# Routing that scatters whole rows with their expert numbers, weights and targets, so that an expert reads its slots in one plain transfer

## What is computed

```python
x = x + jnp.tanh(g_xattn[0]) * _L0_xattn_ref(_layernorm(x, axis=-1), ctx_512, ...)
...
logits = x @ gate_w.T
topv, topi = jax.lax.top_k(logits, TOP_K)
rw = jax.nn.softmax(topv.astype(jnp.float32), axis=-1).astype(x.dtype)
W = jnp.zeros((N, E), x.dtype).at[jnp.arange(N)[:, None], topi].set(rw)
gu = jnp.einsum('nh,eih->nei', x, gu_w)
gate, up = (gu[..., :I], gu[..., I:])
inter = jax.nn.silu(gate) * up
inter_w = inter * W[:, :, None]
out = jnp.einsum('nei,ehi->nh', inter_w, dp_w)
```

## Time and profile before

| | us |
|---|---|
| median of 3 runs | 1684.83 |
| lowest, highest | 1680.01, 1685.89 |
| span of the profiled execution, first to last instruction | 1675.0 |
| between that span and the median of the runs | 9.8 |
| PE busy in the span | 1460.0 |
| DVE busy | 1118.3 |
| POOL busy | 967.6 |
| ACT busy | 677.6 |

### The profile page before, as it was taken

The page is one execution under the profiler, slowest core; times in us unless marked ns, Lnnn a source line. Parts: engine busy times, 40 slices in busy tenths (PEclk is TensorE's granted clock), DMA queues, the critical chain, the costliest instruction groups (busy, mean ns, idle before and its releaser), DMA issues.

```text
span 1675.0 us, 24705 instructions
## 1 busy us (share of the span) xinstructions
PE 1460.0 (87%) x7674; PEld 1183.0 (71%) x7674; DVE 1118.3 (67%) x2420; ACT 677.6 (40%) x1558; POOL 967.6 (58%) x997
## 2 busy tenths in 40 slices
PE   7998899999999999899999899745887888889884
PEld 5766787776787777687777687634777777778742
DVE  5777780588784388796189784543665676767386
ACT  3333670111772011484011372302665666666420
POOL 4654670277773266674267773365877776777321
PEclk9999999999999999999999999866998998999998
DMA  7898204555103665201655504335788999899596
GB/s 249 298 315 280 81 6 135 189 175 170 42 6 97 181 186 176 61 16 51 186 182 170 176 7 129 107 90 166 216 260 271 321 318 297 295 306 282 173 424 291
DMA packets 155974, 308.99 MB, mean 184 GB/s; under 512 B 37626, under 2 KB 73044, under 8 KB 154004
## 3 DMA queue, kind: packets, MB, share of 16 engines
q1 hardware_dynamic: 124100, 245.42, 45.0%
q0 software_dynamic: 31744, 61.99, 12.2%
HBM read 239.01 MB, written 70.43 MB: 185 GB/s over the span
## 4 chain that ended last, share of the span: by engine, by line
PE 53%; DVE 14%; issue 10%; POOL 7%; DMA 7%; ACT 4%; another core or an unknown queue 4%; SPq 1%; POOLq 0%; DVEq 0%; ACTq 0%
PE bank L722 14%; PE bank L724 13%; PE bank L723 13%; PE bank L820 6%; PE bank L846 3%; DMA p_in<-parts 3%; DVE q_sin L1135 2%; POOL parts L1825 2%; DVE q_rope L1131 2%; POOL x_g L1818 1%; DMA x_g<-xn_dram,t_rows 1%; POOL q_rope L1743 1%; PE bank L985 1%; ACT prob L1515 1%
## 5 line engine op out<-in xcount | busy, mean ns | idle before, releaser
L1743 POOL TENSOR_TENSOR q_rope<-q_rope,q_sin 128x448 f32<-128x448 f32 x192 | 218.0, 1164 | 149.4 <-DVE q_sin L1135 148.3
L1749 POOL TENSOR_TENSOR prob<-prob,row_inv 128x375 f32<-128x375 f32 x219 | 176.9, 814 | 105.1 <-DVE row_inv L1157 102.7
L1825 POOL DMA_INDIRECT parts<-y_sb,t_rows x140 | 161.0, 1150 | 84.1 <-ACT y_sb L1651 47.7
L1818 POOL DMA_INDIRECT x_g<-xn_dram,t_rows x140 | 158.0, 1129 | 50.7 <-issue 41.4
L1764 POOL DMA_INDIRECT table<-entry,pos_i x128 | 127.2, 993 | 97.0 <-DVE count L1245 66.3
L820 PE MATMUL bank<-q_rope,m_w 128*128 128x448 f32 x384 | 159.5, 552 | 13.9 <-DVE q_tl L1141 9.1
L1135 DVE TENSOR_TENSOR q_sin<-bank,sin_q 128x448 f32<-128x448 f32 (+1 forms) x256 | 158.1, 618 | 4.0
L1149 DVE TENSOR_REDUCE row_max<-bank 128x1 f32<-128x375 f32 x224 | 119.5, 535 | 41.2 <-PE bank L724 40.6
L846 PE MATMUL bank<-ident,prob 128*125 128x128 f32 x672 | 115.8, 283 | 21.2 <-POOL prob L1749 9.7
L1651 ACT ACTIVATE y_sb<-bank,t_rows 112x512 f32<-112x512 f32 (+5 forms) x140 | 91.4, 687 | 106.0 <-PE bank L724 49.2
L1515 ACT ACTIVATE prob<-bank,row_max 128x375 f32<-128x375 f32 x224 | 128.4, 574 | 9.9 <-DVE row_max L1149 9.4
(11 more groups left out here) (345 smaller groups left out, 4452.2 us busy)
## 6 DMA issues: line engine op xcount, KB each, us to landing
w_ex<-in_w_ex SPq DMA_DIRECT2D x64, 768.0 KB
p_in<-parts SPq DMA_DIRECT2D x14, 2048.0 KB, 16.8
m_w<-m_dram SPq DMA_DIRECT2D x48, 192.0 KB, 2.5
wq_s0h<-wq_dram SPq DMA_DIRECT2D x24, 256.0 KB
wq_s0l<-wq_dram SPq DMA_DIRECT2D x24, 256.0 KB
wq_s1h<-wq_dram SPq DMA_DIRECT2D x24, 256.0 KB
wq_s1l<-wq_dram SPq DMA_DIRECT2D x24, 256.0 KB
wcq_s0h<-wcq_dram SPq DMA_DIRECT2D x24, 192.0 KB
```

Of the source, the lines that this page charges most:

```text
L1743: pool.tensor_tensor(o[:, c, :], o[:, c, :], q_sin[:, c, :], ALU.add).then_inc(s_radd, 1)
L1749: pool.tensor_tensor(prob[i][:], prob[i][:], row_inv[:, i:i + 1].to_broadcast([P, L]), ALU.mult)\
L1818: pool.indirect_dma_start(x_g[x % NXE][0:size, t, :], None, xn2_dram, bass.IndirectOffsetOnAxis(ap=t_rows[x % NROW][0:size, t, 0:1].bitcas ...
L1825: pool.indirect_dma_start(parts, bass.IndirectOffsetOnAxis(ap=t_rows[x % NROW][0:size, t, 1:2].bitcast(I32), axis=0), y_sb[x % NY][t][0:si ...
```

## The change

`table`, the gathers and the table reads go. `slot_rows` in DRAM has 1792 slots for each expert, each a row of 544 words: the 512 channels, the token's eight expert numbers twice, its eight weights, and its eight rows in `parts` (counted from 1280). The routing writes these words into the row buffer (`rows`, three buffers and two `early_rows`) beside the normalised channels, and each of the 8 indirect DMAs of a batch scatters the whole rows of 2176 B to the slots of one choice. The slots must hold zeros before: GpSimd clears `blank` [96, 544], and SP copies it over the first 288 slots of each expert, 64 transfers of 627 KB, at two of three tiles of the attention of passes 0 and 1, each no earlier than ten tiles ahead of the scores. Batches 0 and 1, which were scattered between the heads of pass 1, are scattered behind its attention.

An expert's slots are then read by SP in one plain transfer (`load_slots`), five experts ahead. DVE finds the expert's own weight and target in each row (`find_own`): it compares the row's numbers with the expert's, multiplies, sums over the eight, and sends empty slots to a spare row of `parts`. ACT takes the weight from `own`, and `put` the targets from `to_row`. The eight experts with 3 tiles of 92 slots get 96. The loop behind the experts is changed in the same way. DVE's routing of a batch has one operation less.

```diff
+SPAN = B * S
 TR = 96
-KINDS = ((4, 96, 3), (8, 92, 3), (8, 128, 2), (12, 120, 2), (16, 112, 2), (8, 104, 2), (8, 96, 2))
+KINDS = ((12, 96, 3), (8, 128, 2), (12, 120, 2), (16, 112, 2), (8, 104, 2), (8, 96, 2))
...
+ID_AT, W_AT, TO_AT, RW = C, C + 2 * TOP, C + 3 * TOP, C + 4 * TOP
+SPARE = 1280
...
+NROWS = 3
+BEHIND_FILL = (0, 1)
+FILL_AT = [t for t in range(4, 52) if t % 3]
+FILL_LEAD = 10
...
-NE, NROW, NXE, NY, NC = 3, 12, 5, 3, 4
-NG_AHEAD, NROW_AHEAD = 4, 5
+NE, NROW, NXE, NY, NC = 3, 6, 5, 3, 4
...
-    whole = {"turn": at + 2, "router": at + 4, "choose": at + 5, "rank": at + 7, "place": at + 8,
-             **{f"scatter {k}": at + 9 + k for k in range(TOP)}}
+    whole = {"turn": at + 2, "router": at + 4, "choose": at + 5, "rank": at + 7, "place": at + 8}
+    if g:
+        whole.update({f"scatter {k}": at + 9 + k for k in range(TOP)})
...
-        xn2_dram = nc.dram_tensor("xn2_dram", [B * S + CAP, C], F32).ap()
-        table = nc.dram_tensor("table", [E * SPAN, 3], F32).ap()
-        parts = nc.dram_tensor("parts", [YR + E * CAP, C], F32).ap()
+        xn2_dram = nc.dram_tensor("xn2_dram", [B * S, C], F32).ap()
+        slot_rows = nc.dram_tensor("slot_rows", [E * SPAN, RW], F32).ap()
+        parts = nc.dram_tensor("parts", [SPARE + YR, C], F32).ap()
...
+        with ExitStack() as fill_ctx:
+            blank = fill_ctx.enter_context(nc.sbuf_tensor("blank", [TR, RW], F32))
+            early_rows = [fill_ctx.enter_context(nc.sbuf_tensor(f"early_rows{i}", [S, RW], F32)) for i in range(2)]
...
-        xn2 = [sb(f"xn2{i}", [S, C]) for i in range(2)]
+        rows = [sb(f"rows{i}", [S, RW]) for i in range(NROWS)] + early_rows
...
+                sp.wait_ge(s_zero, 16 * E)
+                for b in BEHIND_FILL:
+                    sp.wait_ge(s_slots[row_buffer(b)], 16 * TOP)
+                    sp.wait_ge(s_xn2_st[row_buffer(b)], 16)
...
-            def load_table():
-                sp.dma_start(table, a["c_table"]).then_inc(s_zero, 16)
-                sp.dma_start(xn2_dram[B * S:, :], a["c_pad_rows"]).then_inc(s_zero, 16)
+            def fill_slots(n, tile):
+                if n == 0:
+                    sp.wait_ge(s_blank, 1)
+                sp.wait_ge(s_score, tile)
+                sp.dma_start(slot_rows[n * SPAN:n * SPAN + CAP, :].rearrange("(p t) w -> p t w", t=CAP // TR),
+                             blank[:].unsqueeze(1).to_broadcast([TR, CAP // TR, RW])).then_inc(s_zero, 16)
...
-                        if g == 0 and t == 4:
-                            load_table()
+                        if g < 2 and t in FILL_AT:
+                            fill_slots(g * len(FILL_AT) + FILL_AT.index(t), max(1, g * GB * RT + t - FILL_LEAD))
...
-            def load_rows(x):
+            def load_slots(x):
                 e = sp.value_load(order[0:1, x:x + 1], min_val=0, max_val=E - 1)
                 size, n = TILES[x]
-                if x >= NROW:
-                    sp.wait_ge(s_put[(x - NROW) % NY], 16 * rows_put(x - NROW))
-                sp.dma_start(t_rows[x % NROW][0:size, 0:n, :], table.rearrange("(e m) w -> e m w", m=SPAN)
+                if x >= NXE:
+                    sp.wait_ge(s_et, FIRST[x - NXE + 1])
+                    sp.wait_ge(s_own, 3 * (x - NXE) + 1)
+                sp.dma_start(x_g[x % NXE][0:size, 0:n, :], slot_rows.rearrange("(e m) w -> e m w", m=SPAN)
                              [bass.ds(e, 1), 0:size * n, :].rearrange("one (p t) w -> p (one t) w", t=n))\
-                    .then_inc(s_rows[x % NROW], 16)
+                    .then_inc(s_xg[x % NXE], 16)
...
-            for x in range(NROW_AHEAD):
-                load_rows(x)
+            for x in range(NXE):
+                load_slots(x)
+            sp.dma_start(spare[:], a["c_spare"]).then_inc(s_spare, 16)
             for x in range(E):
-                if x + NROW_AHEAD < E:
-                    load_rows(x + NROW_AHEAD)
+                if x + NXE < E:
+                    load_slots(x + NXE)
...
+                dve.tensor_scalar(row[:, W_AT:TO_AT], raised[:], small[:, 3:4], None, ALU.mult).then_inc(s_route, 1)
+                dve.tensor_scalar(row[:, TO_AT:RW], own_row[:], float(b * S * KY), None, ALU.add).then_inc(s_route, 1)
...
-                    if b >= 2:
-                        dve.wait_ge(s_xn2_st[b % 2], 16 * (b // 2))
-                        dve.wait_ge(s_x2tr, b - 1)
+                    i, earlier = row_buffer(b), row_before(b)
+                    if earlier is not None:
+                        dve.wait_ge(s_x2tr, earlier + 1)
+                        dve.wait_ge(s_xn2_st[i], 16 * row_uses(earlier))
+                        dve.wait_ge(s_slots[i], 16 * TOP * row_uses(earlier))
...
+            def find_own(x):
+                size, n = TILES[x]
+                row = x_g[x % NXE][0:size, 0:n, :]
+                if x == 0:
+                    dve.wait_ge(s_order, 2)
+                    dve.wait_ge(s_spare, 16)
+                if x >= NROW:
+                    dve.wait_ge(s_put[(x - NROW) % NY], 16 * rows_put(x - NROW))
+                dve.wait_ge(s_xg[x % NXE], 16 * (x // NXE + 1))
+                dve.wait_ge(s_own, 3 * x)
+                dve.scalar_tensor_tensor(found[0:size, 0:n, :], row[:, :, ID_AT:W_AT], order_f[0:size, x:x + 1],
+                                         row[:, :, W_AT:RW], ALU.is_equal, ALU.mult).then_inc(s_own, 1)
+                dve.wait_ge(s_own, 3 * x + 1)
+                dve.tensor_reduce(own[x % NROW][0:size, 0:n, :].rearrange("p t a -> p (t a)"),
+                                  found[0:size, 0:n, :].rearrange("p t (a k) -> p (t a) k", a=2), AX_X, ALU.add)\
+                    .then_inc(s_own, 1)
+                dve.wait_ge(s_own, 3 * x + 2)
+                first = x % NY * 3
+                dve.tensor_tensor(to_row[x % NROW][0:size, 0:n], own[x % NROW][0:size, 0:n, 1],
+                                  spare[0:size, first:first + n], ALU.max).then_inc(s_own, 1)
...
                 if x + 1 < E:
                     turn(x + 1)
+                    find_own(x + 1)
                     split_expert(x + 1)
...
+                act.wait_ge(s_own, 3 * x + 2)
                 for t in range(tiles):
                     act.wait_ge(s_down, FIRST[x] + t + 1)
                     act.activation(y_sb[x % NY][t][0:size, :], bank[5 + t][0:size, :], ACT.Copy,
-                                   scale=t_rows[x % NROW][0:size, t, 2:3]).then_inc(s_y, 1)
+                                   scale=own[x % NROW][0:size, t, 0:1]).then_inc(s_y, 1)
...
+                    i = row_buffer(b)
                     if k % (TOP // 2) == 0:
                         pool.wait_ge(s_route, NR * b + R_POS)
-                        pool.wait_ge(s_zero, 32)
-                    pool.indirect_dma_start(table, bass.IndirectOffsetOnAxis(ap=pos_i[b % 2][:, k:k + 1], axis=0),
-                                            entry[b % 2][:, k, :], None).then_inc(s_tab[b % 2], 16)
+                        pool.wait_ge(s_zero, 16 * E)
+                    pool.indirect_dma_start(slot_rows, bass.IndirectOffsetOnAxis(ap=pos_i[i][:, k:k + 1], axis=0),
+                                            rows[i][:], None).then_inc(s_slots[i], 16)
...
-                for b in held(g if g < NG - 1 else NG):
+                for b in (*(BEHIND_FILL if g == 1 else ()), *held(g if g < NG - 1 else NG)):
...
-            def gather(x):
-                size, tiles = TILES[x]
-                pool.wait_ge(s_rows[x % NROW], 16 * (x // NROW + 1))
-                if x >= NXE:
-                    pool.wait_ge(s_et, FIRST[x - NXE + 1])
-                for t in range(tiles):
-                    pool.indirect_dma_start(x_g[x % NXE][0:size, t, :], None, xn2_dram, bass.IndirectOffsetOnAxis(
-                        ap=t_rows[x % NROW][0:size, t, 0:1].bitcast(I32), axis=0)).then_inc(s_xg[x % NXE], 16)
-
             def put(x):
                 size, tiles = TILES[x]
+                pool.wait_ge(s_own, 3 * (x + 1))
...
-            for x in range(NG_AHEAD):
-                gather(x)
             for x in range(E + 1):
-                if x + NG_AHEAD < E:
-                    gather(x + NG_AHEAD)
                 if x >= 1:
                     put(x - 1)
```

184 lines of the change are left out of this document (102 added, 82 removed).

## The result

The changed kernel takes 1642.67 us, the median of runs from 1640.48 to 1643.64. The kernel before took 1684.62 beside it (1680.01 to 1685.89). The ratio is 0.9757, with a 95% interval from 0.9731 to 0.9784: 42 us less.

A forecast was written before the change was run, and what follows sets the result against it. TensorE, busy 87% of the span, was taken to bound the kernel, GpSimd mattering only where TensorE waits for it. Terms -7 - 11 + 0 - 10 + 3 + 1 = -24 us took 1684.8 to 1661, range 1628 to 1692.

The forecast's parts named there:

- rival 1: Whole kernel at 1639 us: plain reads move faster than 2-KB gathers, middle 29 experts -15, other 35 -7; chance 0.18.
- Start, -7: Start of the experts: first transpose 8 us earlier, 1 us added for scatters, together -7; bounds 0 and -12.
- under 10: Sign in the experts: PE's wait for `x_g` falls from 45.9 us to under 10.
- 8 us, 1143, about where the first gate product ends: Start of the experts: four slot loads, then `spare`, 2.5 MB, take 8 us, to about the first gate product's end.
- First 19, -11: First 19 experts: 6.8 us each, 129 us for 140, so -11; bounds 0 and -15.
- Middle 29, 0: Middle 29 experts: 6.1 us each at the same DMA rate, no gain; bounds +3 and -8.
- Last 16, -10: Last 16 experts: 5.6 us each, 90 us for 100, so -10; bounds -3 and -14.
- `find_own`: DVE in the experts: 192 small instructions, 0.6 us an expert, costed at nothing beside DMA; bounds 0.45 and 1.0.
- The fill, +3: Attention of passes 0 and 1: zero fills fit at 2.33 us each with little room, +3; bounds -3 and +38.
- rival 3: Whole kernel slower, 1699 us: fills of 3.3 us hold up the attention of passes 0 and 1, +38; chance 0.15.
- Scatters of batches 0 and 1, 0 and +1: End of pass 1: sixteen scatters, 20 us, covered by idle times, 0; +1 beside `project_out`'s loads.
- Rival 2: Experts: the 16 DMA engines set the pace in all three groups, only the start is won, 1682 us; chance 0.17.

The follow-up runs named there:

- the first pair: First profiles of the kernel before and the changed kernel, nothing else changed: spans 1675.0 and 1640.3 us.
- e4: Kernel before with 12 experts of 3 x 96 slots, 8 of them 3 x 92 until then, gathers kept: 1613.1 us where before takes 1634.7, ratio 0.9869.
- e3: Changed kernel with context ahead of fills, sixteen scatters spread over pass 2's heads, `spare` ahead of slots: 1619.75 us where before takes 1634.7, ratio 0.9912.
- f3: Changed kernel with context ahead of fills and `spare` ahead of slots, sixteen scatters left in a row: 1622.8 us where before takes 1685.2, ratio 0.9639.
- the second pair: Profiles of f2 (changed kernel) against f1 (kernel before) from another set of runs, differing by 52.1 us; medians differ by 44.
- e1: Changed kernel with the next batch's context asked for ahead of the fills in passes 0 and 1: 1615.7 us where before takes 1634.7, ratio 0.9873.
- g3: f3 with the sixteen scatters issued one by one in the attention of pass 2: 1621.4 us where before takes 1634.65, ratio 0.9913.
- f4: e4 with the context asked for at tile 0 of a batch in passes 0 and 1: 1680.65 us where before takes 1685.2, ratio 0.9968.
- h1: Changed kernel plus 140 unneeded POOL gathers of 16-byte rows, waiting only for those two experts back: 1707.6 us where before takes 1679.2, ratio 1.0181.
- g1: Changed kernel, unchanged, run again where before takes 1634.65 us: 1635.0 us, ratio 1.0006.
- f1: Kernel before, unchanged, run again for its profile where before takes 1685.2 us: 1684.9 us, ratio 0.9997.
- f2: Changed kernel, unchanged, run again where before takes 1685.2 us: 1640.9 us, ratio 0.976.
- g2: Changed kernel plus 140 unneeded POOL gathers of 16-byte rows, waiting for the previous expert's: 1749.7 us where before takes 1634.65, ratio 1.0722.

## Why the prediction was right, and where not

The forecast was 1661 in 1628 to 1692, faster at 0.68. It came out faster, at 1642.7, inside the range and near the time of rival 1 (1639), but for other reasons than rival 1's. The direction and the places of the gain were right. The number owes something to luck: in the first pair 58 us are won where 28 were forecast and 23 lost where 4 were, and the two errors partly cancel. And on chip L the same forecast would have failed, since there the change is worth nothing. Step by step:

- **Start, -7.** The first transpose comes 3.5 to 4 us earlier behind tile 220, and 3.5 to 4.5 behind the last scatter, less than the 6 to 9 said. PE's wait there is still 20.5 us, so the sign "under 10" failed; with 25.5 before and 8 won it could not have held. But the first tanh follows after 7.1 us in place of 17.9, since the next experts' rows lie there too and no gather chain stands between; in the first profile of before ACT also has 12.4 us of "remote" there, and e4, without any, takes 11.6. -14.3 together: undersized, beyond my bound of -12. It would be some 7 more with `spare` ahead of the slots (e3, f3). "8 us, 1143, about where the first gate product ends" was the step that failed there: `spare` came behind five slot loads of 627 KB, 9.7 us after its issue, and DVE, which had halves to make, stood for it.
- **First 19, -11.** It is -22. My floor of 6.8 us an expert was too high: the steady pace is 6.3 us for three tiles and 5.1 to 5.2 for two of 128 rows. PE is full (58.0 of 58 us). The range of 0 to -15 was too narrow also because I took the slowness of before for POOL's order alone (8.7 us an expert). That order is real: POOL's queue is as good as full in e4, which needs 120.0 us for these 19. The other 20 us of before are there on chip H alone, with the late signals that stood in the profile as "remote" and that I did not see.
- **Middle 29, 0.** +1.2 in the first pair. The weights' and rows' bytes bind there (DMA share 1.02). Right; but the second pair has -17 and chip L some +16 against e4, so a zero was one case of three. e4 moves 335 GB/s there with its gathers, at the same DMA share of 1.02, so 309 GB/s was no limit.
- **Last 16, -10.** The last group, counted over 15 intervals, is -17.4, beyond my -14; the undisturbed pace there is 4.7 us, not 5.6. Mechanism as said, size off for the same reason as in the first 19.
- **`find_own`.** 0.6 us an expert and no visible cost, as said.
- **The fill, +3.** This is the step that failed by most: +14 and +9 in the two pairs. The bandwidth was judged rightly (264 to 270 GB/s beside the attention). What was misjudged is the queue: I let the "12 us of lead" hide the context's load, but SP issues a fill in some 2 us when its queue is full, so the load is issued late (191.32 for a read at 200), and then stands behind four fills of about 2.3 us. These are the signs of rival 3, POOL's waits for `kv_raw` and a longer attention, at a third of its price and with another cause: rival 3 had the fill itself slow. One moved line cures it (e1).
- **Scatters of batches 0 and 1, 0 and +1.** +5.8 and +11.0 on chip H behind pass 1. On POOL they fit into the idle times of the earlier trace rows, as said. The cost is in the signals of another engine, which I did not count. On chip L it is about 3 (g3). From tile 112 to 220 the changed kernel is 3.3 and 1.5 us slower; why isn't shown.
- **The end**, which I did not touch, is 5 us shorter. 3 of them come with the table of tiles (92.5 and 92.7 us behind the last put in e4 and f4, 95.6 in the kernel before); the rest is open.

Rival 1's own sign, over 330 GB/s in the middle, is not there in the first pair (322); in the second it is just reached (330), but e4 has 335 with gathers, so that rate is no merit of plain reads. Rival 2 (transfers bind anyway, 1682) was given by a page of the Trainium skill, "DMA: Bandwidth & Descriptors", section "Issuing engines are not separate DMA queues": another issuer saves only issue time, which is usually small. Here it isn't small: with its gathers POOL's queue is full in e4, and in h1 gathers that move next to nothing cost 67 us. On chip L the outcome of the rule is still what one gets, ratio 1.0006: there POOL is freed, and the DMA share of 1.02 in the middle 29 stays. For the rows, the Trainium skill ("DMA: Bandwidth & Descriptors", section "Why a DMA increments its semaphore by 16 and not by 1") says that a transfer goes over the largest number of engines, at most 16, that divides the slowest dimension of both its sides, some direct copies excepted. Worked out from that, an estimate, it is 4 engines for 92 rows and 16 for 96. e4's 22 us agree in direction; the profiles don't show which engine moved a packet, and f4 finds nothing of it on chip H.

**What stays open.** Why PE's signals are late, and PE is slowed, on chip H and not on L. Shown is only that late signals stand where POOL issues indirect transfers in a row, with bytes or without, in all seven profiles with the times of H and in none of the seven from chip L. How the 67 us of h1 divide between POOL's full queue, puts that land late, and late signals; and so how much of the 42 us is each. What the idle gathers of h1 cost on chip L. Where the kernel before spends its time on chip L, of which there is no profile. And that L and H are two kinds of chip rests on four sets and the first comparison.

## What to carry to other kernels

A plain transfer in place of indirect ones can pay where the issuing engine sends them without pause. Look for two signs: its own work with the pause ahead of each transfer fills the stretch, and the waits of the *other* engines have "remote" or "issue" in them. Before an edit that moves big transfers into a quiet stretch, list the small loads that share the queue, and move those ahead. Repeat a gain of 2% on another chip before it is called one: this one was 0.976 on one and 1.001 on another, while the version with the context first and `spare` first (f3) has 0.964 where before takes 1685, and e1, the first of its two repairs, 0.987 where it takes 1635. There one changed line in the table of the kernel before (e4) gives as much, 0.987.

## What the runs showed of the hardware

- The same program, the kernel before, ran at 1679 to 1685 us on some chips and at 1635 on others, and by its version with 96 rows (f4, e4) the difference is in the experts; the changed kernel, with half the indirect transfers there, ran at 1635 to 1643 on both.
- During sixteen indirect scatters in a row, signals that TensorE sent reached ScalarE 8.6 us and VectorE 9.9 us behind the work that sends them, on the one kind of chip; on the other, with the same program (g1), no such wait is in the profile.
- While GpSimd issued indirect transfers without a pause (h1), eight transposes of TensorE that take 1.04 us otherwise were spread over 10 us. TensorE's idle time that nothing in the profile explains is 10 to 33 us in the experts of before, f1, f4 and h1, and none in those of e4, f2, g1 and g2.
- 140 indirect gathers of 16 bytes a row, which hardly anyone waits for directly (POOL 1.2 us), cost 67 us on the one kind of chip. They cost GpSimd 1.27 us each and 0.3 us ahead of each.
- SP's issue of a 627 KB fill takes about 2 us when transfers are queued (8.06 us for four at 455.9); a small load that stands behind them is issued late for that reason alone.
